# Attention kernel with second-pass scores on 64-row tiles, one fp16 shift row, and query rows fetched by DMA

## What is computed

```python
def _L0_xattn_ref(q_x, k_x, v_x, energy_coeffs, Wq, bq, Wk, bk, Wv, bv, Wo, bo):
    ...
    Q = proj(q_x, Wq, bq)
    K = proj(k_x, Wk, bk)
    V = proj(v_x, Wv, bv)
    scores = jnp.einsum('bhqd,bhkd->bhqk', Q, K) / np.sqrt(Dh).astype(np.float32)
    attn = jax.nn.softmax(scores, axis=-1)
    ...
```

## Time and profile before

| what | value |
|---|---|
| median of two executions | 2006.35 us |
| span of the profiled execution (first to last instruction) | 2004.8 us |
| longer of the two executions timed | 2006.69 us |
| PE busy | 1839.7 us (92%) |
| DVE busy | 1427.8 us (71%) |
| ACT busy | 1217.7 us (61%) |
| POOL busy | 146.3 us (7%) |

### The profile page before, as it was taken

How to read it: one execution, slowest core, us unless ns; L and a number is a source line. 1 busy time by engine, 2 the same in 40 slices (tenths; PEclk the granted TensorE clock), 3 DMA queues, 4 the chain that set the end, 5 groups by cost and what they waited for, 6 DMA issues and landing times.

```text
span 2004.8 us, 43706 instructions
## 1 busy us (share of the span) xinstructions
PE 1839.7 (92%) x14449; PEld 800.7 (40%) x14449; DVE 1427.8 (71%) x2650; ACT 1217.7 (61%) x2194; POOL 146.3 (7%) x239
## 2 busy tenths in 40 slices
PE   6699999977779999997897999999789999999978
PEld 4333333345222333333574233333344444444445
DVE  6688888647878888883685888888457666666448
ACT  3177777742435777775793577777534566565636
POOL 5000000012000000002121000000000000000012
PEclk9899999989998999998898899999988999999979
DMA  9711111105111111110115111111051111111001
GB/s 259 231 36 51 36 52 35 59 1 171 35 44 45 44 44 43 44 35 22 43 54 174 44 45 44 44 44 35 33 174 36 36 35 35 35 35 35 20 6 38
DMA packets 78783, 116.81 MB, mean 58 GB/s; under 512 B 16823, under 2 KB 50958, under 8 KB 78702
## 3 DMA queue, kind: packets, MB, share of 16 engines
q1 hardware_dynamic: 75326, 106.84, 17.9%
q0 software_dynamic: 2432, 7.94, 1.3%
q10 hardware_dynamic: 944, 0.93, 0.1%
HBM read 81.12 MB, written 34.23 MB: 58 GB/s over the span
## 4 chain that ended last, share of the span: by engine, by line
PE 82%; DVE 8%; ACT 3%; DMA 3%; issue 2%; POOL 1%; SPq 1%; DVEq 0%; ACTq 0%; POOLq 0%
PE pv_bank L1420 23%; PE exp_ring L1402 22%; PE score_ring L1389 18%; PE exp_ring L1406 5%; DVE mx L997 3%; PE score_ring L1566 3%; PE exp_ring L1577 3%; DMA k_d<-k2c 2%; PE score_ring L1331 1%; ACT early L771 1%; PE exp_ring L1338 1%; PE score_ring L1479 1%; DMA qp<-ms 1%; DVE stats L913 1%; PE score_ring L1370 1%
## 5 line engine op out<-in xcount | busy, mean ns | idle before, releaser
L771 ACT ACTIVATE early<-exp_ring 128x512 f32<-128x512 f32 (+1 forms) x1728 | 970.7, 596 | 485.1 <-PE exp_ring L1402 303.1
L997 DVE TENSOR_REDUCE mx<-score_ring 128x1 f32<-128x800 f32 (+2 forms) x896 | 784.5, 907 | 163.2 <-PE score_ring L1389 151.2
L1402 PE MATMUL exp_ring<-qp,kp 128*128 128x512 f16 (+1 forms) x1728 | 623.1, 387 | 7.3 <-DMA qp<-ms 6.9
L1389 PE MATMUL score_ring<-kp,qp 128*128 128x400 f16 (+2 forms) x2176 | 573.8, 345 | 43.3 <-DVE mx L997 22.9
L1420 PE MATMUL pv_bank<-early,vg 128*32 128x256 f32 (+1 forms) x6912 | 555.1, 391 | 1.8 <-ACT o_all L760 0.9
L1402 PEld LDWEIGHTS exp_ring<-qp,kp 128*128 128x128 f16 (+1 forms) x1728 | 149.2, 98 | 397.1 <-ACT early L771 279.8
L1389 PEld LDWEIGHTS score_ring<-kp,qp 128*128 128x128 f16 x2176 | 208.8, 99 | 238.8 <-DVE mx L997 86.0
L1420 PEld LDWEIGHTS pv_bank<-early,vg 128*32 128x32 f32 (+1 forms) x6912 | 139.2, 108 | 270.3 <-issue 157.8
L1406 PE MATMUL exp_ring<-mask_eye,mask 128*128 128x256 f16 (+1 forms) x832 | 159.2, 273 | 0.0
L1406 PEld LDWEIGHTS exp_ring<-mask_eye,mask 128*128 128x128 f16 (+1 forms) x832 | 82.3, 99 | 59.0 <-issue 0.7
L607 POOL COPY vg<-v_all 128x416 f32 (+1 forms) x48 | 25.4, 533 | 1030.6 <-PE pv_bank L1420 983.1
(11 more groups left out here) (231 smaller groups left out, 1162.7 us busy)
## 6 DMA issues: line engine op xcount, KB each, us to landing
kp<-k_d SPq DMA_DIRECT2D x128, 400.2 KB, 3.1
k_d<-k1c SPq DMA_DIRECT2D x32, 400.2 KB, 7.0
ctxT<-ctxT_d SPq DMA_DIRECT2D x12, 800.5 KB, 6.2
k_d<-k2c SPq DMA_DIRECT2D x16, 400.2 KB, 7.6
qp<-q_d SPq DMA_DIRECT2D x320, 12.0 KB
k_d<-v_loc POOLq DMA_DIRECT2D x12, 400.2 KB, 9.2
ctxT_d<-ctxT SPq DMA_DIRECT2D x4, 800.5 KB, 7.4
o_all<-in_ctx SPq DMA_DIRECT2D x4, 768.0 KB
```

The lines of the kernel that those rows point to most:

```text
L771: act.activation(pt[g][0:rows_, 2 * h:2 * h + 2, :], bank[0:rows_, :].rearrange("p (i q) -> p i q", q=S), ACT.Exp).then_inc(exped, 1)
L997: dve.tensor_reduce(dst, src, AX.XY, ALU.max).then_inc(score_free, 1)
L1389: ins = pe.matmul(pa[slot][:, z, 0:w], qp1[par][:, i, qt * P:qt * P + P], kp1[par][:, at:at + w], start=True, stop=True)
L1402: ins = pe.matmul(bank[0:rows_, :], kp2[par][:, s * P:s * P + rows_], qp2[par][:, 2 * h:2 * h + 2, :], start=True, stop=True, skip_group_c ...
```

## The change

- Second pass: each fill now uses only the 64 rows of its two heads, rows 0 to 63 for h = 0 and 64 to 127 for h = 1. The first pass stays on all 128 rows. The mask matmuls stay on 128 rows.
- The maxima are one fp16 number instead of a high and a low part: one shift row per pair of heads (row 24 for heads 0 and 1, row 88 for heads 2 and 3). On DVE a unit's `split_maxima` with its five instructions becomes `keep_maxima` with one (two in the masked run).
- The copy qp1 to qp2 is gone. SyncE loads the four heads' query rows for the second pass from q_d, four more DMAs per unit, and the maxima go in two DMAs instead of one. SyncE waits for `m_ok` in place of `q_kept`.
- In the unmasked runs a piece holds two heads and one chunk of keys instead of one head and two chunks; DVE reduces it to two maxima. In the local run there are 4 pieces of two matmuls instead of 8 of one.
- Two more memsets (qp2) at the program's start.

```diff
-KM = KQ + 2
+KM = KQ + 1
...
-        return [(0, w + 1, 2), (2 * w + 1, w, 2)]
-    return [(0, nk, 1)]
+        return [(0, w + 1), (w, w + 1), (2 * w + 1, w), (3 * w + 1, w)]
+    return [(0, nk)]
...
-        self.turn, self.ahead = (2, 9) if self.local else (3, 7)
+        self.turn, self.ahead = (2, 5) if self.local else (3, 7)
...
-        self.c = QT * HG * len(self.chunks)
+        self.c = QT * PAIRS * len(self.chunks)
...
+    def step(self, j):
+
+        n = len(self.chunks)
+        if self.mask:
+            qt, c, i = j // (2 * HG), j // HG % 2, (0, 2, 1, 3)[j % HG]
+            return qt, [(i, 2 * c), (i, 2 * c + 1)]
+        qt, c, m = j // (PAIRS * n), j // PAIRS % n, j % PAIRS
+        return qt, [(m, c), (PAIRS + m, c)]
...
             def pass2(r, n, par):
                 sp.dma_start(kp2[par][:, 0:r.nk], k_d[r.index][n]).then_inc(in2[par], 16)
+                for i in range(HG):
+                    sp.dma_start(qp2[par][R * i:R * i + KQ, i, :], q_d[r.layer][n, R * i:R * i + KQ, :]
+                                 ).then_inc(in2[par], 16)
...
-                    sp.dma_start(qp2[par][KQ:KQ + 2, :, :], ms[par][:, :]).then_inc(m_in[par], 16)
+                    for h in range(PAIRS):
+                        lo = 2 * R * h + KQ
+                        sp.dma_start(qp2[par][lo:lo + 1, 2 * h:2 * h + 2, :], ms[par][2 * h:2 * h + 2, :]
+                                     ).then_inc(m_in[par], 16)
...
-                    sp.wait_ge(q_kept, r.u0 + n + 1)
+                    sp.wait_ge(m_ok, r.u0 + n + 1)
...
-                        dve.tensor_reduce(dst, src, AX.XY, ALU.max).then_inc(score_free, 1)
...
+                        dst = mx[par][:, qt * HG:qt * HG + HG, c].rearrange("p (z m) -> p z m", z=2)[:, :, i]
+                        dve.tensor_reduce(dst, src, AX.X, ALU.max).then_inc(score_free, 1)
...
-                    split_maxima(n, par, first)
-                    if r.local:
-
-                        dve.wait_ge(fill, r.fill0 + (n - 1) * r.fills)
-                    dve.tensor_copy(qp2[par][:, :, :], qp1[par][:, :, :]).then_inc(q_kept, 1)
+                    keep_maxima(n, par, first)
...
-                    ins = pe.matmul(bank[0:rows_, :], kp2[par][:, s * P:s * P + rows_],
-                                    qp2[par][:, 2 * h:2 * h + 2, :], start=True, stop=True, skip_group_check=r.mask)
+                    half = slice(2 * R * h, 2 * R * h + 2 * R)
+                    ins = pe.matmul(bank[0:rows_, :], kp2[par][half, s * P:s * P + rows_],
+                                    qp2[par][half, 2 * h:2 * h + 2, :], start=True, stop=True, skip_group_check=r.mask)
...
-                                    piece(n + d, (par + d) % 2, k)
+                                    piece(n + d, (par + d) % 2, k, half=1 - h)
```

More of the change, by code:

```diff
@@ L212, in flamingo @@
         pt = [m[:, 0, :, :] for m in early_mem]
[L213 removed]
+        mx = [sb(f"mx_{i}", [P, QT * HG, 4]) for i in range(2)]
         nm = [sb(f"nm_{i}", [P, QT, HG]) for i in range(2)]
[L215 to L217 removed]
+        m16 = [sb(f"m16_{i}", [P, QT, HG], F16) for i in range(2)]
+        ms = [sb(f"ms_{i}", [HG, S], F16) for i in range(2)]
         mask01 = sb("mask01", [P, QT, S2], F16)
@@ L857, in _ @@
             dve.memset(v_all[:, :, FULL, :], 0.0).then_inc(dconst, 1)
-            for m in qp1:
+            for m in qp1 + qp2:
                 dve.memset(m[:, :, :], 0.0).then_inc(dconst, 1)
@@ L895, in weights @@
                 dve.tensor_copy(mask01[:, :, :], mask8[:, :, :]).then_inc(prep_v, 1)
[L896 to L900, removed]
+                for c, (lo, w) in enumerate(chunk_cols(S2)):
+                    dve.tensor_scalar(mask_add[:, :, c, 0:w], mask8[:, :, lo:lo + w], -BIG, None, ALU.mult
+                                      ).then_inc(prep_v, 1)
                 dve.wait_ge(prep_v, 11)
@@ L977, in attention @@
             def attention(r):
-                cpt = len(r.chunks)
+                cpt = 2 if r.mask else len(r.chunks)
                 def piece(n, par, k, j, first):
[L982 to L985, removed]
+                    qt, ((i, c), _) = r.step(j)
+                    w = r.chunks[c][1]
+                    src = pa[r.slot(par, k, first)][:, :, 0:w]
                     dve.wait_ge(score, r.use(n, k, first) + 1)
@@ L999, in split_maxima, with keep_maxima @@
-                def split_maxima(n, par, first):
+                        dst = mx[par][:, qt * HG:qt * HG + HG, c].rearrange("p (z m) -> p z m", z=2)[:, :, i]
+                        dve.tensor_reduce(dst, src, AX.X, ALU.max).then_inc(score_free, 1)
+                def keep_maxima(n, par, first):
                     dve.wait_ge(score_free, FREE_SCORE + r.use(n, r.uses - 1, first) + 1)
[L1001 to L1010, removed]
-                                      ALU.subtract).then_inc(m_ok, 1)
@@ new lines, in keep_maxima @@
+                    if r.mask:
+                        dve.tensor_reduce(nm[par][:, :, :].rearrange("p q i -> p (q i)"), mx[par][:, :, 0:cpt], AX.X,
+                                          ALU.max, negate=True).then_inc(mx_done, 1)
+                        dve.wait_ge(mx_done, n + 1)
+                        dve.tensor_scalar(m16[par][:, :, :], nm[par][:, :, :], -MIN_MAX, None, ALU.min
+                                          ).then_inc(m_ok, 1)
+                    else:
+                        dve.tensor_reduce(m16[par][:, :, :].rearrange("p q i -> p (q i)"), mx[par][:, :, 0:cpt], AX.X,
+                                          ALU.max, negate=True).then_inc(m_ok, 1)
@@ L1369, in turn, with piece @@
                     for qt in range(QT):
-                        ins = pe.transpose(pa[slot][:, 0, :].bitcast(F16)[0:2 * HG, qt * P:qt * P + P],
-                                           m16[par][:, qt, :, :].rearrange("p a i -> p (a i)"), ident16[:, :])
+                        ins = pe.transpose(pa[slot][:, 0, :].bitcast(F16)[0:HG, qt * P:qt * P + P],
+                                           m16[par][:, qt, :], ident16[:, :])
                     ins.then_inc(score, 1)
-                def piece(n, par, k, first=False):
+                def piece(n, par, k, first=False, half=0):
                     use, slot = r.use(n, k, first), r.slot(par, k, first)
                     if k == r.turn:
-                        pe.wait_ge(m_ok, 2 * (r.u0 + n))
+                        pe.wait_ge(m_ok, r.u0 + n)
                         turn(1 - par, slot, use)
@@ L1384, in piece @@
                         pe.wait_ge(in1[par], IN_DMAS * (r.u0 + n - par + 2))
-                    qt, c, i = j // (cpt * HG), j // HG % cpt, j % HG
-                    lo, w, nb = r.chunks[c]
-                    for z in range(nb):
-                        at = lo + z * (S2 // 4)
+                    qt, banks = r.step(j)
+                    w = r.chunks[banks[0][1]][1]
+                    for z in (half, 1 - half):
+                        i, c = banks[z]
+                        at = r.chunks[c][0]
                         ins = pe.matmul(pa[slot][:, z, 0:w], qp1[par][:, i, qt * P:qt * P + P],
```

16 lines of the change are left out of this document (7 added, 9 removed).

## The result

The changed kernel takes 2171.23 us (median of 2 runs, 2163.66 and 2178.8), 1.083 times the kernel before (95% interval 1.079 to 1.0871). The forecast was 2141.5 in a range of 2055 to 2240. Its profiled execution is the one of 2163.66 us, span 2161.8 against 2004.8 before: +157 us, where the sum of the terms had +135.

The account below looks back on a forecast made before the run. The prediction took PE's stream to bound four of five runs, with the local run waiting for the maxima's DMA. Terms 167 - 40 + 10 - 2 = +135 us on 2004.8 gave 2140, so 2141.5 at the median, range 2055 to 2240.

Parts of the forecast that it names:

- Term 1: PE's stream between fills, pieces and mask matmuls: 1673 added changes of tile at 0.10 us each, +167 us.
- Rival 1: PE's fills: the change of rows is free and 64-row tiles bring only overlap; 1974 us, chance 0.17.
- rival 2: PE's changes of tile: each costs the full wait of 0.17 us; 2259 us, chance 0.10.
- rival 3: PE's neighbouring fills don't overlap, so the gain from pairs falls away; 2182 us, chance 0.08.
- Term 2: Neighbouring fills in unmasked runs may run together: 222 pairs at 0.18 us each, -40 us.
- Term 3: Local run: SyncE's queue of twelve issues becomes the limit at about 6.0 us a unit, +10 us.
- Rival 4: PE streams less and its granted clock falls to 1.2 GHz for stretches, priced on masked units; 2260 us, chance 0.03.
- Term 4: Run starts: DVE's five instructions become one, while the first fill waits for both maxima DMAs; net -2 us.
- Edits at nothing: Long runs' saved DVE instructions and second maxima DMA are hidden; query loads and memsets also cost nothing.

Follow-up runs that it names:

- e1: Changed kernel with second-pass fills back on all 128 rows, everything else kept; 2017.71 us, ratio 1.0046 to the kernel before.
- e2: Changed kernel with both fills of a step issued side by side, then mask matmuls, pieces, product; 1956.99 us, ratio 0.9743 to the kernel before.
- e3: Changed kernel with the pieces of the unmasked runs on 64-row tiles too, masked run left alone; 1952.28 us, ratio 0.9722 to the kernel before.
- after: The changed kernel itself, against the kernel before; 2171.23 us, ratio 1.083.
- e4: Changed kernel with DVE copying qp1 to qp2 in all runs in place of four query DMAs per unit; 2183.04 us, ratio 1.0864 to before.
- e5: Changed kernel with fills on 128 rows in the local run alone; 2157.07 us, ratio 1.0762 to the kernel before.
- e6: e5 plus, in the local run only, DVE copying the query rows in place of four DMAs; 2147.73 us, ratio 1.0723 to the kernel before.
- b1: Changed kernel with 64-row pieces and fills in unmasked long runs, fills before masks in the masked run, 128-row local run; 1857.85 us, ratio 0.9278 to before.
- b2: b1 plus DVE's copy of the query rows in the local run; 1839.59 us, ratio 0.9179 to the kernel before.

## Why the prediction was right

- **Term 1, changes of tile at 0.10.** Right in count and price. The two weak points were that the price came from changes of columns and that the trace had none of rows. Both directions of rows measure 0.10 (fill to piece 0.32, piece to fill 0.45), the masked unit gives 4.07 / 39 = 0.104, and e1, e2 and e3 remove the changes in three ways and lose their cost each time. Rival 1 (free) and rival 2 (0.17) fall; rival 3 (no overlap) falls at 737.40. The Trainium skill, "TensorEngine Tiling (Array Packing)", section Tiling Modes, Key Properties, has a change of the mode drain the engine, and the trace agrees, for rows as for columns. The factor of up to two, which the prediction put in the same section, stands in section Theoretical Speedup of that page of the Trainium skill; it shows here where neighbours keep one mode, as in the pair of fills at 737.40 and in e3.
- **Term 2, 0.18 per pair.** The sum was right and its reason wrong. I held that loading the second fill's weights would cost 0.04; the second fill is free (0.22), and the ring takes 0.19 back from the pair behind a step without a piece. Of a unit's five pairs that is one: 5 x 0.22 - 0.19 = 0.91, where 5 x 0.18 is 0.90. That the two agree is luck. 24 x 0.10 - 5 x 0.18 came out at 1.5 against 1.57 measured.
- **Term 3, the local run, +10.** It is +20.6, and the step that failed is "So SyncE's queue becomes the limit, at about 6.0 us". First the term was mis-sized: between the first and the last copy of the maxima e1 takes 95.3 us against 79.5, 15.8 more, because the gaps in the queue are 1.2 us a unit and not 0.5 (my upper end, 6.4 us and +17, had it). Second, in the changed kernel another limit lies above it: at 1.2 GHz PE takes 6.66 us a unit, 99.9 us, 4.6 more. Rival 4 named this clock, but I priced it only for the masked run, where it didn't happen (and with a unit of 24.7 us, the stretch of the earlier trace rows divided by 16, where the unit is 25.62); I had asked how full PE's stream is and not looked at the lightly loaded run.
- **Term 4 and the run starts.** From a long run's first piece to its first copy of the maxima the changed kernel takes 0.5 to 1.1 us less, near the 0.9 forecast, but the totals per run don't show it apart. Run 2's start spent 13.6 us more at half clock, which no term had, and the run lost 5.4 us more than forecast.
- **Edits at nothing.** e1 holds them all, but for the local run: the unmasked and masked units are within 0.03 us of before. So the single shift row, the second DMA of the maxima and the queries by DMA were hidden in the long runs, as argued.

The forecast lay 30 us under the median, of which some 8 are the slower of two executions and nearly all the rest the local run (10.6), run 2's start (5.4) and the masked run (3.9, its changes at 0.104). The forecast held because terms 1 and 2, which make 127 of the 135 us, came out.

Left open: what makes the clock stay low in the local run beyond that it is 0.50 with 64-row fills (after, e3, e4), 0.67 with the same fills side by side (e2), and 0.84 or more with 128-row fills (e1, e5, e6, b1, b2); and why some starts of a run lose 8 us more than others. That the two executions of the changed kernel differ by 15 us goes with their mean clocks of 0.928 and 0.917, and two such starts would be 16 us; the second one was not profiled, so this was not shown.

## What to carry to other kernels

Before you narrow a matmul's tile, write down the tile shapes in PE's order and count the places where they change; each cost 0.10 us here, nearly half of a 512-column fill, and hand-made interleaving with other shapes turned a free second matmul into a loss of 8%. Group matmuls of one shape, or bring their neighbours to the same shape: in b2 the 64-row fills of the long runs then gave a gain of 8%. And price each stage at the clock that it will get, the quiet stages too: here the local run, which had waited for a DMA, ran at 1.2 GHz with 64-row fills and became bound by PE.

## What the runs showed of the hardware

- A change between 64*128 and 128*128 costs 0.10 us in both directions (0.32 against 0.22), and the same 0.10 at 1.2 GHz (0.54 against twice 0.22): it did not double with the granted clock halved.
- Two matmuls on different halves of the rows cost one (0.22 us for 2 x 512 columns), and the two need not belong to the same operation: a fill and a piece started together at 705.51 (e3).
- In the local run the clock was 0.50 for 80 us with PE busy 79 of 80 at that clock (after, e4), and 0.86 with PE busy 48 of 75 (e5), the only difference of e5 from the changed kernel being the rows that its local fills use. At starts of unmasked runs the half clock lasted up to 44 us and cost some 8 us in some runs and not in others, only in kernels whose 64-row fills stand between 128-row pieces (after, e4, e5, e6).
- Twelve DMA issues on SyncE's queue took 5.3 us a unit and 1.2 us of gaps, and set the local unit at 6.5 us (e1, e5).
